# Query and key projections placed in the drain, the first norm's residual sums on TensorE, and the experts' bias products ahead of the norm

## The reference

```python
x = x + attn(layernorm(x))            # causal, windows of 64, 16 heads of 8
x = x + xattn(layernorm(x), ctx)      # keys and values by bucket weights, 16 heads of 8
y0 = layernorm(x)
qkv = y0 @ w.T + b                    # the third part: 4 heads of 32; attention runs over
scores = q @ k.T / sqrt(32)           # the 16 batches at one position, 128 positions
o = softmax(scores) @ v
y1 = ln(y0 + o @ ow.T + ob) * g1 + be1
gates = softmax(y1 @ wg); idx = argmax(gates)            # 8 experts
h = disp @ w1[e] + b1[e]; y = h @ w2[e] + b2[e]          # no activation between the two
moe = where(place < 256, gate * y[idx], 0)
x = x + ln(y1 + moe) * g2 + be2
```

## Time and profile before

| | |
|---|---|
| executions shown | 363.73, 366.38, 366.94 us (median 366.38) |
| the profiled execution | 364.65 us |
| its span, first to last instruction | 362.6 us |
| busy share of the span | TensorE 89%, VectorE 74%, ScalarE 44%, GpSimd 34% |
| the chain that ended last, by engine | TensorE 79%, VectorE 6%, ScalarE 4%, waits of issue 4% |
| granted TensorE clock, mean | 0.959 |

### The profile page before, as it was taken

How to read it: one execution, slowest core, us unless ns; L and a number is a source line. 1 busy time by engine, 2 the same in 40 slices (tenths; PEclk the granted TensorE clock), 3 DMA queues, 4 the chain that set the end, 5 groups by cost and what they waited for, 6 DMA issues and landing times.

```text
span 362.6 us, 12236 instructions
## 1 busy us (share of the span) xinstructions
PE 324.4 (89%) x4742; PEld 218.8 (60%) x4742; DVE 269.5 (74%) x689; ACT 159.4 (44%) x429; POOL 123.4 (34%) x197
## 2 busy tenths in 40 slices
PE   7649998999999999999999999888998699689992
PEld 3225565666666665656565655675665239689991
DVE  6756789666667999999999988364554277959994
ACT  2114474555566655556465656421543312203331
POOL 1074543000000545563324442362000022404996
PEclk9896999999999999999999999999999996589998
DMA  8950413454482265995910000000000000216101
GB/s 217 261 146 32 150 44 102 123 151 124 153 209 81 64 146 156 188 242 172 221 28 3 2 4 2 5 2 2 2 2 4 0 0 3 83 38 231 32 30 58
DMA packets 36584, 31.80 MB, mean 88 GB/s; under 512 B 4792, under 2 KB 33480, under 8 KB 36400
## 3 DMA queue, kind: packets, MB, share of 16 engines
q1 hardware_dynamic: 34240, 27.42, 27.4%
q0 software_dynamic: 1280, 3.15, 3.3%
q10 hardware_dynamic: 1008, 0.46, 0.5%
HBM read 23.32 MB, written 7.70 MB: 86 GB/s over the span
## 4 chain that ended last, share of the span: by engine, by line
PE 79%; DVE 6%; issue 4%; ACT 4%; DMA 3%; POOL 2%; SPq 1%; POOLq 0%; DVEq 0%
PE ps L1238 9%; PE ps L1558 9%; PE ps L1184 9%; PE ps L1221 9%; DMA ctx_sorted<-room 3%; PE ps L1194 3%; PE ps L1137 3%; PE ps L1158 3%; PE ps L1305 3%; PE ps L1271 3%; PE ps L1150 3%; ACT pT L1033 2%; PE ps L1381 2%; PE ps L1478 2%; PE ps L1128 2%
## 5 line engine op out<-in xcount | busy, mean ns | idle before, releaser
L914 ACT ACTIVATE pT<-ps 128x512 f32<-128x512 f32 x128 | 73.7, 609 | 81.3 <-PE ps L1194 75.5
L792 POOL TENSOR_TENSOR rstd<-veps,minus_half 128x1 f32<-128x1 f32 x32 | 19.2, 600 | 115.4 <-DVE veps L432 115.4
L467 DVE TENSOR_REDUCE m_pad<-ps 128x8 f32<-128x1024 f32 x32 | 39.1, 1220 | 16.2 <-PE ps L1221 16.2
L443 DVE TENSOR_TENSOR p_sb<-qk_sb,heads 128x512 f32<-128x512 f32 x64 | 44.0, 687 | 1.6 <-DMA ident_bf<-c_ident_bf 1.2
L470 DVE TENSOR_REDUCE m_pad<-ps 128x8 f32<-128x1024 f32 x32 | 38.9, 1215 | 0.0
L857 POOL TENSOR_TENSOR rs<-ve,half 128x2 f32<-128x2 f32 x16 | 13.9, 871 | 73.1 <-DVE ve L670 72.9
L1221 PE MATMUL ps<-p_sb,qk_sb 32*128 32x512 f32 x256 | 38.4, 671 | 0.0
L1184 PE MATMUL ps<-p_sb,qk_sb 32*128 32x512 f32 x256 | 37.1, 644 | 0.0
L1558 PE MATMUL ps<-mexp,pT 128*128 128x128 f32 x256 | 33.4, 286 | 1.8 <-DVE room L774 1.2
L1238 PE MATMUL ps<-pT,p_sb 128*32 128x128 f32 x1024 | 34.6, 276 | 0.0
L1558 PEld LDWEIGHTS ps<-mexp,pT 128*128 128x128 f32 x256 | 31.5, 200 | 2.5 <-DVE pT L748 1.6
(11 more groups left out here) (189 smaller groups left out, 671.6 us busy)
## 6 DMA issues: line engine op xcount, KB each, us to landing
room<-mask_rows SPq DMA_DIRECT2D x32, 128.0 KB, 3.7
wkv_sb<-wkv SPq DMA_DIRECT2D x23, 128.0 KB, 2.0
kv_sorted<-room SPq DMA_DIRECT2D x5, 512.0 KB, 3.2
w1t_sb<-w1t SPq DMA_DIRECT2D x8, 256.0 KB, 4.1
w_sb<-w SPq DMA_DIRECT2D x8, 256.0 KB, 4.9
kv_sb<-hot_rows SPq DMA_DIRECT2D x4, 512.0 KB, 4.4
ctx_sorted<-room SPq DMA_DIRECT2D x1, 1472.0 KB, 12.1
tk<-fside SPq DMA_DIRECT2D x1, 1024.0 KB
```

Of the source, the lines that this page charges most:

```text
L443: return dve.tensor_tensor(dst, rows.unsqueeze(1).broadcast_to([128, QUADS, S]), heads[:, 0, :].unsqueeze(2).broadcast_to([128, QUADS, S]) ...
L467: dve.tensor_reduce(m4[:, 0:2, 0:QUADS], ps[:, 0:2, :].rearrange("p g (j k) -> p g j k", j=QUADS), AX.X, ALU.max).then_inc(s["max_low"], 1)
L792: pool.tensor_tensor(rstd[:, :], veps[:, :], minus_half[:, :], ALU.pow)\
L914: act.activation(pT[:, t % 2, g, :, :], quad[4 + g], ACT.Exp).then_inc(s["exped"], 1)
```

## The change

Four things are moved and two are computed on other engines.

- `turn_sorted(i + 1)` and its copy now stand in period i, after the output projection on TensorE and after the group's copies on ScalarE, one period ahead; group 0 stays where it was.
- `mha_project` takes four batches instead of a quarter of the groups: its moving operand is a view of `y0T` in runs of 8 elements, and its results are written to `qT` and `kT` in the same runs. Three of the four pairs stand in the drain (`QK_PERIODS`), the fourth where the first stood. The experts' products move by a period or two, and the scaling of the query weights moves from period T to T-2.
- In the first norm the residual is added on TensorE: a second product, of the identity with y0, into the same bank, and four banks instead of three. Statistics and scaling then read PSUM.
- The experts' bias products stand in a wait of the attention (`first_biases`, eight products with 32 rows of result in four column groups), then `expert_biases` on VectorE keeps what belongs together, and `expert_rows` spreads it before the first norm. The blocks are made by ScalarE (`bias_blocks`, 16 operations) and no longer by GpSimd.
- `route_picks(0)` and `gated(0)` stand one batch later, `place(0)` after `ffn(0)`, and the last store goes out on ScalarE's queue.

```diff
-EXPERT_PERIODS = (T - 1, T, T + 2, T + 4)
+EXPERT_PERIODS = (T - 1, T + 1, T + 3, T + 4)
+QK_PERIODS = (T, T + 2, T + 4)
...
+        def four_batches(rows, i):
+            return rows.rearrange("p g (b j) -> p b g j", j=NPOS)[:, 4 * i:4 * i + 4]
...
-                if p == T:
+                if p == T - 2:
                     dve.wait_ge(s["ffn_w_in"], 16 * nloads[0])
                     dve.tensor_scalar(inw_sb[:, 0:D], inw_sb[:, 0:D], MHD ** -0.5, None, ALU.mult)
...
+            def expert_biases(h):
+                dve.wait_ge(s["cb_done"], h + 1)
+                dve.tensor_tensor(b1w2[:, 4 * h:4 * h + 4, :], quad[h],
+                                  pick_expert[:, 4 * h:4 * h + 4].unsqueeze(2).broadcast_to([128, 4, D]), ALU.mult)
...
             def z_stats(b, k):
+                if k == 0:
+                    dve.wait_ge(s["f_proj_done"], b + 1)
+                    dve.bn_stats(st16[:, b, :], bank[b % 4][:, 0:D]).then_inc(s["st_step"], 1)
...
             def first_norm(b):
-                if b < B:
-                    dve.wait_ge(s["y0_biased"], b + 1)
-                    dve.wait_ge(s["f_proj_done"], b + 1)
-                    dve.tensor_tensor(z16[:, b, :], y0[:, b, :], bank[b % 3][:, 0:D], ALU.add)
...
-                if b == 13:
+                if b == 14:
                     route_picks(0)
-                if b == 16:
+                if b == 17:
                     gated(0)
...
+            def bias_blocks():
+                act.wait_ge(s["crep_done"], 1)
+                act.copy(crep[:, :], bank[3][:, 0:128]).then_inc(s["crep_copied"], 1)
+                act.wait_ge(s["crep_copied"], 1)
+                for b in range(B):
+                    act.activation(cblk[:, b, :], crep[:, :], ACT.Identity, scale=batchof[:, b:b + 1])
...
+            act.wait_ge(s["last_rows"], 2)
+            act.dma_start(out[B - 2:B].rearrange("b s d -> s b d"), y0[:, B - 2:B, :]).then_inc(s["stored"], 16)
...
                 if sort_group(t - 1) is not None:
-                    pe.wait_ge(s["srtT_copied"], sort_group(t - 1) + 1)
+                    pe.wait_ge(s["srtT_copied"], min(sort_group(t - 1) + 2, SORT_GROUPS))
...
+            def mha_project(i, a):
+                if i == 0:
+                    pe.wait_ge(s["w_ffq_ready"], 2)
+                    pe.wait_ge(s["exped"], 4 * T)
+                else:
+                    pe.wait_ge(s["k_ready" if a else "qT_ready"], i)
+                pe.wait_ge(s["f_xT_copied"], 4 * i + 4)
+                pe.matmul(bank[6 + a], inw_sb[:, a * D:(a + 1) * D], four_batches(y0T, i),
+                          start=True, stop=True).then_inc(s["k_done" if a else "q_done"], 1)
...
+            def first_biases(h):
+                for c in range(FC):
+                    mm = pe.matmul(quad[h][group(c)], b1t_sb[:, c, :], w2_sb[:, 4 * h:4 * h + 4, c, :],
+                                   start=True, stop=True, skip_group_check=True)
+                mm.then_inc(s["cb_done"], 1)
+            def expert_rows():
+                pe.wait_ge(s["b1w2_ready"], 2)
+                for e in range(E):
+                    pe.matmul(bank[3][:, 0:128], pick_expert[:, :], b1w2[:, e, :], start=(e == 0), stop=False)
...
+                    if m >= 4:
+                        pe.wait_ge(s["w_ready"], m - 3)
+                    pe.matmul(bank[m % 4][:, 0:D], aT[:, m, :], ow_sb[:, :], start=True, stop=False)
+                    pe.wait_ge(s["y0_biased"], m + 1)
+                    pe.matmul(bank[m % 4][:, 0:D], ident[:, :], y0[:, m, :], start=False, stop=True)
```

More of the change, by code:

```diff
@@ L128, in decoder_kernel @@
                     for i in range(2))
-        lnden, rdens = (p_sb[:, i, 0:2, :, :].rearrange("p u r k -> p u (r k)") for i in range(2))
+        rdens, lnden = (p_sb[:, 1, 2 * i:2 * i + 2, :, :].rearrange("p u r k -> p u (r k)") for i in range(2))
         vaug = loop_room[:, 2048:4096].rearrange("p (u h c) -> p u h c", u=4, h=H)
@@ L375, in _ @@
             hot_to_all(1)
-            for i in range(B // 2):
-                if i < B // 2 - 1:
-                    sp.wait_ge(s["out_rows"], 2 * i + 2)
-                else:
-                    sp.wait_ge(s["last_rows"], 2)
+            for i in range(B // 2 - 1):
+                sp.wait_ge(s["out_rows"], 2 * i + 2)
                 sp.dma_start(out[2 * i:2 * i + 2].rearrange("b s d -> s b d"), y0[:, 2 * i:2 * i + 2, :])\
@@ L675, in z_scaled @@
                 dve.wait_ge(s["mv_step"], B * (k + 1) + b + 1)
[L676 removed]
+                src = bank[b % 4][:, 0:D] if k == 0 else z16[:, b, :]
+                dve.scalar_tensor_tensor(z16[:, b, :], src, mv16[:, b, 0:1], scale, ALU.subtract, ALU.mult)\
                    .then_inc(s["w_ready"], 1)
@@ L992, in _ @@
                     turn_max(p + 1)
-                if sort_group(p) is not None:
-                    copy_sorted(sort_group(p))
+                if sort_group(p) == 0:
+                    copy_sorted(0)
                 if live(p):
@@ L1008, in _ @@
                     kvs_copy(sort_group(p))
+                    if sort_group(p + 1) is not None:
+                        copy_sorted(sort_group(p + 1))
                 if p in EXPERT_PERIODS:
                     expert_copy(EXPERT_PERIODS.index(p))
+                if p in QK_PERIODS:
+                    mha_queries(QK_PERIODS.index(p))
                 if 0 <= p - Y0_TURN < B:
                     y0T_copy(p - Y0_TURN)
-            act.wait_ge(s["ffn_w_in"], 16 * nloads[0])
-            act.wait_ge(s["w_ffq_ready"], 2)
-            def mha_queries(i):
-                act.wait_ge(s["q_done"], i + 1)
-                act.activation(qT[:, 4 * i:4 * i + 4, :], quad[4 if i == 0 else 0], ACT.Identity, bias=inb_col[:, 0:1])\
-                   .then_inc(s["qT_ready"], 1)
             def mha_turned_max(i):
@@ L1343, in _ @@
                     turn_max(p + 1)
-                if sort_group(p) is not None:
-                    turn_sorted(sort_group(p))
+                if sort_group(p) == 0:
+                    turn_sorted(0)
                 if p == -2:
@@ L1355, in _ @@
                 if sort_group(p) is not None:
+                    if sort_group(p + 1) is not None:
+                        turn_sorted(sort_group(p + 1))
                     sorted_kv(sort_group(p), p)
@@ L1375, in _ @@
             pe.wait_ge(s["exped"], 4 * T)
-            def mha_project(i, a):
-                if i >= 1:
-                    pe.wait_ge(s["f_max_low"], i)
-                pe.matmul(bank[(4 if i == 0 else 0) + a], inw_sb[:, a * D:(a + 1) * D], y0T[:, 4 * i:4 * i + 4, :],
-                          start=True, stop=True).then_inc(s["k_done" if a else "q_done"], 1)
             def mha_project_v(i):
                 for r in range(QUADS):
-                    mm = pe.matmul(quad[6 if i == 0 else 2][:, r, :], y0T[:, 4 * i + r, :], inw_sb[:, 2 * D:3 * D],
+                    mm = pe.matmul(quad[5 if i == 0 else 2][:, r, :], y0T[:, 4 * i + r, :], inw_sb[:, 2 * D:3 * D],
                                    start=True, stop=True)
@@ L1618 @@
         "w1t": a["L0_ffn_w1"].transpose(0, 2, 1),
-        "b1t": a["L0_ffn_b1"].T,
+        "b1t": _np.concatenate([a["L0_ffn_b1"].T, _np.zeros((FF, 32 - E), _np.float32)], axis=1),
         "w2": a["L0_ffn_w2"],
@@ L1636 @@
     arrays["c_sort"] = _np.broadcast_to(row, (128, 112)).astype(_np.float32)
-    rows = _np.eye(E)[:, None, None, :] * _np.eye(E)[:, :, None, None]
-    rows = _np.concatenate([rows, rows.sum(axis=1, keepdims=True)], axis=1)
-    arrays["c_pick_expert"] = _np.broadcast_to(rows, (E, E + 1, B, E)).reshape(E, E + 1, 128).astype(_np.float32)
+    arrays["c_pick_expert"] = (p[:, None] % 32 == p[None, :] % E).astype(_np.float32)
     arrays = {k: _np.ascontiguousarray(v) for k, v in arrays.items()}
```

135 lines of the change are left out of this document (57 added, 78 removed).

## The result

| | before | after |
|---|---|---|
| executions, us | 363.73, 366.20, 366.38, 366.94 | 353.51, 354.49, 355.05, 356.92 |
| median | 366.29 | 354.77 |
| the profiled execution | 364.65 | 355.05 |
| its span | 362.6 | 353.2 |

The ratio estimated from these runs is 0.9733, with an interval of 0.9678 to 0.9789 (the quotient of the two medians, 0.969, lies inside it): faster, by 8 to 12 us. The forecast was 355.8, and on another chip, on which the kernel before took 369.0, the changed kernel came to 359.1, a ratio of 0.9751 (0.9711 to 0.9790).

A forecast was written before the change was run, and what follows sets the result against it. TensorE, holding 79% of the chain of waits, was taken as the bound. The terms -1.8 + 0.2 + 5.1 - 3.5 + 0.7 - 8.95 - 0.6 = -8.85 took 364.65 to 355.8 us; range 352.0 to 361.5.

The forecast's parts named there:

- a norm of over 25 to the last logits: First norm: a stated sign that the forecast is wrong, the norm needing over 25 us to its last logits.
- late fall: Norm's end: clock falls between 14.5 and 20.2, while TensorE has few products; +2.4, giving 355.8; chance 0.43.
- Sorting, -1.8: Loop's sorting periods: wait before sorted products goes in five of six, period 6 waits about 0.4; -1.8, between -0.6 and -1.8.
- T-2, +0.2: Period T-2: scaling of query weights now stands ahead of the spreading of queries that TensorE waits for; +0.2.
- drain, +5.1: Drain: three projection pairs come in, +5.7, and cover one wait of 0.61; +5.1, between +4.8 and +5.7.
- the rival of 371: Projections: strided moving operand in runs of 32 bytes costs extra; at three times the price 371; chance 0.04.
- Attention, -3.5: Attention: three pairs, 5.7, leave, but transposes of maxima then wait for VectorE; -3.5, between -3.0 and -4.0.
- Pause, +0.7: Attention's last waits: bias products, 2.1, hidden in 2.19; nine spreading products, 2.0, in a wait of 1.30; +0.7.
- Norm, -8.95: First norm: VectorE sets the pace, 2.0 a pair; -11.35 if the clock stays high, -8.95 with its late fall.
- Clock falls early, 363.8: Norm: clock falls early and stays low, 1.5 a batch, TensorE sets the pace; 363.8; early or halfway fall 0.10.
- GpSimd's lock: Norm: power starts only after the rows, a pair 2.1 instead of 2.0, 0.7 over the norm; not in the sum.
- Tail, -0.6: Kernel's end: last store leaves ScalarE a microsecond earlier and the seventh ends the span; -0.6, between 0 and -1.

The follow-up runs named there:

- sort_back: Changed kernel with a sorted group's transposes and copy back in their own period; stretch from output projection of period 5 to that of 12: 58.19 us.
- qk_back: Changed kernel with query and key projections back in the attention, a quarter of the groups at a time, contiguous operand; ratio 0.9672 to the kernel before.
- rows_split: Changed kernel with the nine spreading products cut in two, five ahead of the norm, four ahead of batch 4's projection; pause 8.70, norm 24.75 us.
- before_pause: Kernel before with only the bias part: bias products in the attention's pause, rows spread ahead of the norm, blocks on ScalarE; ratio 0.9773.
- pool_blocks: Changed kernel with the 16 bias blocks made by GpSimd again instead of ScalarE; norm 26.12 us against 24.93 unedited.
- last_sp: Changed kernel with the last store back on SyncE's queue behind the seventh; last FFN products to the end 9.28 us.
- idle: Changed kernel with eight idle bf16 products ahead of the turns of batches 13, 14 and 15; ratio 0.9711 to the kernel before, norm 24.40 us.
- split_load: Changed kernel with the load of the later sorted tiles split, second group's four tiles first; stretch from output projection of period 5 to that of 12: 55.11 us.

## Why the prediction was right, step by step

The forecast held: -8.85 predicted for the span, -9.4 measured, of which 1.1 came from the two stretches that no part of the change touches. The stretches that it does touch gave -8.4 in the first trace and -8.8 in the second. That the sum lies this close is in part luck: its terms miss by up to 0.7, sorting one way, pause, norm and tail the other. By one of its own signs of being wrong, a norm of over 25 to the last logits, the first trace even failed: 25.14 up to their start (285.85 to 310.99), 24.50 in the second. That sign lay only 0.3 above the 24.7 that the forecast itself gave the norm with a late fall. By its steps:

- **Sorting, -1.8: too small.** Measured -2.49, -2.36, and -3.07 where the load came early. The five waits go as said and period 6 waits for the load, 0.53 for the forecast 0.4. The term was sized by the recorded idle time, 0.37; the wait cost 0.54, as the recorded end of a product lies behind the point from which the next may start (`sort_back`).
- **T-2, +0.2, and drain, +5.1:** the wait grew by 0.16, and the stretches together by 5.12. Three pairs of 1.9 and one covered wait of 0.6 were the right account, though a wait of 0.35 for the experts' copy came in as well (242.40) and others changed by up to 0.2. The strided operand has no surcharge in these rows, and the rival of 371 did not come.
- **Attention, -3.5:** -3.41, with waits of 1.09 and 0.48 before the transposes of the maxima. `qk_back` gives back the same. That the projections' move costs 1.6 is shown, not only argued.
- **Pause, +0.7: mis-sized.** +1.02. The bias products are hidden, as said. The nine spreading products took 2.40 (283.45 to 285.85), not 2.0, and the stretch that covers them is 1.37, from start to start, for a recorded wait of 1.30. `rows_split` takes the whole of it out.
- **Norm, -8.95:** -8.47 and -9.11. The pace was 2.02 for 2.0, and the case of the late fall came true in every unedited norm. With the clock at full it took 22.67, 11.37 below before; that term was -11.35. The fall itself costs 2.3 to 2.9, forecast 2.4, more when it comes earlier. By parts, the biases brought 7.26 of it (`before_pause`). The stalls are worth the 2 that I had said up to the first FFN product (2.05, `pool_blocks`) and 1.19 at the end of the norm, since the clock comes back in the same place. How the rest divides between products, spreading and clock was not measured.
- **Clock falls early, 363.8:** it did not come, and its price stays open. With the sums on VectorE the clock fell 6.1 behind the first product, and a batch took 1.07. The 1.5 of the rival had the identity product in it; at my 0.22, doubled at the lower level, that makes 1.51, so the 1.07 does not speak against it. With the identity product an early fall was never seen.
- **GpSimd's lock,** priced at 0.7 from what the Trainium skill (SBUF — State Buffer, Who interferes with whom) states: the price is not borne out. The power is recorded 0.17 behind the rows' start, takes 0.74 beside them and 0.71 where no such operation runs, and a pair takes 2.02, not 2.1. I had let the whole power start at the rows' end. The lock itself is not refuted by it. Behind a longer operation of VectorE's with two SBUF inputs, in the FFN, the same power takes 1.67 and ends 0.55 behind that operation (319.73 and 319.18); in the norm it ends 0.56 behind the rows (290.64 and 290.08). So part of the power seems to pass before it needs what VectorE holds, and 0.35 is too short to show; that is inferred from these rows and not tested.

```profile
317.95 1.23 DVE L759 TENSOR_TENSOR pT<-kv_sb,y1T 128x1024 f32<-128x1024 bf16 x1
318.06 1.67 POOL L868 TENSOR_TENSOR rs<-ve,half 128x2 f32<-128x2 f32 x1 [14.38 <-DVE ve L685]
```

- **Tail, -0.6: wrong.** Measured -0.1. The step "the last now leaves ScalarE a microsecond earlier and the seventh ends the span" failed: the end lies 2.9 behind GpSimd's last row in all fourteen traces, whether the eighth store stands behind the seventh or not (`last_sp`), so an earlier issue of the eighth had nothing to gain.
- **Begin, no term:** -0.98 in the first pair of traces. It is scatter: 59.5 to 63.9 in the experiments.

## What to carry to other kernels

Move work into a wait only up to what the wait costs, and price that from start to start: the recorded idle time understates it by the overlap that a wait breaks (0.54 for 0.37), and products that overfill the wait cost what they take beyond it (the spreading, 2.40 in 1.37). Where the clock falls between stages, look for the longest wait ahead of the fall and try to fill it with idle products; here, filling only the waits behind it gained a quarter of what filling it as well did. Work of the engine that bounds the time, moved from one full stage to another (the projections, +1.6), is worth an experiment that takes it back alone, even in a change that wins. And a delay ahead of a low stretch of the clock can look smaller behind it than it is (2.05 against 1.19 in `pool_blocks`): read it where it arises, too.

## What the hardware showed that I had not expected

- The granted clock can fall while TensorE works without a gap: at 310.1 in `idle`, 1.9 behind the end of the wait, with TensorE busy throughout from 309. In the unedited kernel the fall came 15.9 and 18.2 behind the norm's first product, although TensorE's rows from the attention's end up to the earlier fall lie the same to 0.1 in both traces.
- It dips elsewhere too, at other places in each run: 228 to 232 (`split_load`), 263 to 267 (`pool_blocks`), for 1.6 and 1.1 us of time. These dips, and waits of issue such as one of 1.47 at 155.19 (`idle`), belong to the scatter of a run.
- The load of 19 tiles landed in time in one trace of nine and 0.43 to 0.84 late in the others, though it is issued at the same point of the program.
